# New orders for every engine of a two-layer attention and MoE kernel, new PSUM banks, and waits for loads at every step that needs them

## The reference

```python
x = x + L0_xattn(_layernorm(x), ctx, Wq, Wk, Wv, Wo, bo)     # 8 heads of 64
x = x + L0_ffn(_layernorm(x), w_gate, w1_e, w3_e, w2_e, w1_s, w3_s, w2_s)
                                # 16 experts of 64, best 4 within the best 2 of 4 groups; shared: 128
x = x + L1_xattn(_layernorm(x), ctx, Wq, Wk, Wv, Wo)         # 16 heads of 8
x = x + L1_ffn(_layernorm(x), router_w, experts_bias, w1, w3, w2, sw1, sw3, sw2)
                                # 8 experts of 256, best 2 by softmax; shared: 256
```

## Time and profile before

| | us |
|---|---|
| median of 3 runs (lowest to highest) | 231.48 (231.04 to 233.0) |
| span of the profiled execution | 230.0 |
| PE busy | 223.5 (97%) |
| DVE busy | 163.7 (71%) |
| ACT busy | 155.3 (68%) |
| POOL busy | 126.4 (55%) |

### The profile page before, as it was taken

How to read it: one execution, slowest core, us unless ns; L and a number is a source line. 1 busy time by engine, 2 the same in 40 slices (tenths; PEclk the granted TensorE clock), 3 DMA queues, 4 the chain that set the end, 5 groups by cost and what they waited for, 6 DMA issues and landing times.

```text
span 230.0 us, 4315 instructions
## 1 busy us (share of the span) xinstructions
PE 223.5 (97%) x1389; PEld 166.7 (72%) x1389; DVE 163.7 (71%) x480; ACT 155.3 (68%) x378; POOL 126.4 (55%) x127
## 2 busy tenths in 40 slices
PE   7999999999999999999999999999999999999994
PEld 3676765965889898889535563588878887888883
DVE  3589984788667863699948983564857775776874
ACT  2579999986679445672689778876365586745561
POOL 2765743899046937767492107209499400996540
PEclk9999999999999999999999999999999999999999
DMA  6890000000029925900600000028000003700002
GB/s 204 211 296 4 1 3 0 0 3 1 3 74 242 362 114 144 221 3 4 217 3 3 3 1 6 0 79 293 0 0 0 3 0 87 284 0 4 0 0 91
DMA packets 10172, 17.04 MB, mean 74 GB/s; under 512 B 3715, under 2 KB 5540, under 8 KB 9766
## 3 DMA queue, kind: packets, MB, share of 16 engines
q1 hardware_dynamic: 9926, 16.45, 23.5%
q10 hardware_dynamic: 224, 0.32, 0.4%
HBM read 16.08 MB, written 0.62 MB: 73 GB/s over the span
## 4 chain that ended last, share of the span: by engine, by line
PE 86%; ACT 6%; DVE 4%; POOL 2%; issue 1%; DVEq 0%; POOLq 0%
PE psum L1175 12%; PE psum L1179 11%; PE psum L1176 11%; PE psum L1348 7%; ACT prob L749 5%; PE psum L1410 5%; PE psum L1356 4%; PE psum L1358 3%; PE psum L1357 3%; PE psum L1466 3%; PE psum L1294 3%; PE psum L1306 3%; PE psum L1431 2%; PE psum L1270 2%; PE psum L1183 2%; PE psum L1454 2%
## 5 line engine op out<-in xcount | busy, mean ns | idle before, releaser
L703 POOL TENSOR_TENSOR act_s<-act_s,spread 128x512 f32<-128x512 f32 x35 | 44.3, 1293 | 20.2 <-DMA spread<-cw 14.5
L1175 PE MATMUL psum<-xT_hi,w_hi 128*128 128x512 f32 x108 | 43.9, 406 | 0.0
L1179 PE MATMUL psum<-xT_lo,w_hi 128*128 128x512 f32 x108 | 42.3, 392 | 0.0
L1176 PE MATMUL psum<-xT_hi,w_lo 128*128 128x512 f32 x108 | 42.2, 391 | 0.0
L798 ACT CAST q<-psum 128x512 fp32r<-128x512 f32 x35 | 20.4, 587 | 20.4 <-PE psum L1358 14.1
L1009 DVE TENSOR_TENSOR q<-psum,q 128x512 fp32r<-128x512 f32 x35 | 23.8, 687 | 13.5 <-ACT q L798 13.2
L788 ACT ACTIVATE act_s<-psum 128x512 f32<-128x512 f32 x39 | 23.0, 597 | 12.3 <-PE psum L1179 7.7
L1146 DVE TENSOR_REDUCE neg_max<-psum 128x2 f32<-128x308 f32 x64 | 26.2, 472 | 4.3 <-PE psum L1410 4.0
L703 POOL TENSOR_TENSOR hid<-hid,spread 128x512 f32<-128x512 f32 x13 | 16.6, 1296 | 18.9 <-DMA spread<-cw 14.6
L652 POOL TENSOR_TENSOR rstd<-vareps,minus_half 128x4 f32<-128x4 f32 x8 | 8.1, 1017 | 34.0 <-DVE vareps L910 34.0
L646 POOL TENSOR_TENSOR w_lo<-w_src,w_hi 128x768 fp32r<-128x768 f32 x12 | 21.7, 1830 | 8.3 <-ACT w_hi L718 8.3
(11 more groups left out here) (171 smaller groups left out, 469.6 us busy)
## 6 DMA issues: line engine op xcount, KB each, us to landing
spread<-cw SPq DMA_DIRECT2D x16, 256.0 KB, 4.9
spread<-cw SPq DMA_DIRECT2D x6, 512.0 KB, 5.7
w_src<-in_w SPq DMA_DIRECT2D x2, 1152.0 KB, 5.1
w_src<-in_w SPq DMA_DIRECT2D x1, 2304.0 KB, 11.6
spread<-cw SPq DMA_DIRECT2D x8, 128.0 KB, 3.0
w<-in_w SPq DMA_DIRECT2D x1, 576.0 KB, 6.6
out<-X SPq DMA_DIRECT2D x4, 128.0 KB, 1.8
wv<-in_wv SPq DMA_DIRECT2D x2, 192.0 KB, 4.7
```

Source lines behind the costliest of these rows:

```text
L703: pool.tensor_tensor(g, g, spread[:, slot, :], ALU.mult).then_inc(weighed, 1)
L1175: pe.matmul(dst, w_hi, xT_hi[:, b, :], start=True, stop=False)
L1176: pe.matmul(dst, w_lo, xT_hi[:, b, :], start=False, stop=False)
L1179: return pe.matmul(dst, w_hi, xT_lo[:, b, :], start=False, stop=True)
```

## The change

The whole of `PROGRAM` is rewritten: the same steps, in another order on all five engines, and PE's steps in other banks. SP's order differs in two places. In the first MoE layer a load stands ahead of the last of the five spreads of batch 0, and the load for the last layer's w2 stands one place further behind. The transpose of batch 0's expert weights (`cwT`) stood behind both halves of batch 1's `wo` and now stands between them. DVE rounds batch 0's `xT_lo` (`xT`) ahead of the statistics of batch 1's first tiles (the second `lnA`), where it stood behind them. Of the table these lines stand for the rest:

```diff
     "PE":
...
-        "pT.5 pT.3 pT.1 pT.2 k1.7 xT.6 k1.2 pT.4 pT.1 pT.6 gate.3 rest.1.6.4.5 pv pv pv pv h1.4 h1.6 wo.5 " +
-        "wo.1 cwT.3 h1.4 h1.3 h3.1 h3.4 h1.7 h3.1 xT.3 h3.0 h1.6 h3.5 gate.3 h3.7 h3.2 down.4 down down h1.1 " +
...
+        "h1.4 gate.3 pT.7 pT.0 pT.2 h3.6 rest.5.1.7.2 k1.0 pv pv pv pv wo.1 cwT.3 wo.2 h1.7 h1.5 h3.2 h3.4 h1.1 h1.3 " +
...
     "DVE":
-        "lnA sel lnA xT vf1 q q vf xT " + 9 * "score " +
...
+        "lnA xT lnA q q score score xT score score score score score vf1 norm q q score vf1 score score vs norm score " +
...
     "SP":
-        "store spread spread spread spread spread fetch store spread spread spread spread spread place_max " +
-        "fetch place_max place_max place_max store spread spread spread spread spread store spread spread " +
-        "spread spread spread out out out out ",
+        "store spread spread spread spread fetch spread store spread spread spread spread spread place_max place_max " +
+        "fetch place_max place_max store spread spread spread spread spread store spread spread spread spread spread " +
+        "out out out out ",
```

```diff
+        reached = {}
+
+        def need(eng, semaphore, n):
+
+            at = (id(eng), id(semaphore))
+            if n > reached.get(at, 0):
+                eng.wait_ge(semaphore, n)
+                reached[at] = n
+
         def wait_filled(eng, key):
 
             k, n, _ = uses[key]
-            eng.wait_ge(bank_ready[k], n)
+            need(eng, bank_ready[k], n)
...
         def wait_moved(eng, key):
 
-            eng.wait_ge(*reads_of(key))
+            need(eng, *reads_of(key))
...
+                    if s == 2:
+                        wait_moved(dve, ("y", 1, b))
...
                     moved(dve.tensor_tensor(xb, bank(key).rearrange("p (t d) -> p t d", t=T), xb, ALU.add), key)
-                    wait_moved(dve, key)
...
-            def product3(dst, w_hi, w_lo, s, b, first):
-
-
-                if first:
-                    pe.wait_ge(xT_rounded, position[("xT", s, b)])
+            def product3(dst, w_hi, w_lo, s, b):
+
+                need(pe, xT_rounded, position[("xT", s, b)])
                 pe.matmul(dst, w_hi, xT_hi[:, b, :], start=True, stop=False)
                 pe.matmul(dst, w_lo, xT_hi[:, b, :], start=False, stop=False)
-                if first:
-                    wait_moved(pe, ("xT", s, b))
+                wait_moved(pe, ("xT", s, b))
                 return pe.matmul(dst, w_hi, xT_lo[:, b, :], start=False, stop=True)
...
                 elif kind == "pT":
                     b, t, k = step[1:]
                     r = (b * T + t) % 2
-                    if k == 0:
-                        pe.wait_ge(prob_normed, position[("norm", b, t)])
+                    need(pe, loaded["ident"], 16)
+                    need(pe, prob_normed, position[("norm", b, t)])
```

More of the change, by code:

```diff
@@ L1190, in _ @@
                     p = step[1]
-                    if p == 0:
-                        pe.wait_ge(loaded["ctx"], 16 * N_CTX)
+                    need(pe, loaded["ctx"], 16 * N_CTX)
                     filled(pe.matmul(bank(step)[:, 0:B * CP], wk0[:, p * P:(p + 1) * P],
@@ L1195, in _ @@
                 elif kind in ("vf", "vf1", "vs", "vs1"):
+                    need(pe, loaded["ctx"], 16 * N_CTX)
                     if kind in ("vf", "vs"):
-                        if step == ("vf", 0):
-                            pe.wait_ge(loaded["ctxv"], 16)
+                        need(pe, loaded["ctxv"], 16)
                         w, k = wv0, CD
                     else:
-                        if step == ("vf1", 0):
-                            pe.wait_ge(loaded["kv1"], 16 * N_KV1)
+                        need(pe, loaded["kv1"], 16 * N_KV1)
                         w, k = wv1, CD + 1
@@ L1239, in _ @@
                     b, p = step[1:]
-                    if (b, p) == (0, 0):
-                        pe.wait_ge(lo_of["wq0"], 1)
+                    need(pe, lo_of["wq0"], 1)
                     c = slice(p * P, (p + 1) * P)
-                    filled(product3(bank(step), wq_hi0[:, c], wq_lo0[:, c], 0, b, p == 0), step)
+                    filled(product3(bank(step), wq_hi0[:, c], wq_lo0[:, c], 0, b), step)
                 elif kind == "scores":
@@ L1311, in _ @@
                     wait_moved(pe, ("xT", s, b))
-                    if (s, b) == (1, 0):
-                        pe.wait_ge(lo_of["gates"], 1)
+                    need(pe, lo_of["gates"], 1)
                     w = 2 * EXPERTS[s]
@@ L1332, in _ @@
                         pe.wait_ge(lo_of[name], w // CHUNK + 1)
-                    filled(product3(bank(step), hi[:, w, :], lo[:, w, :], s, b, False), step)
+                    filled(product3(bank(step), hi[:, w, :], lo[:, w, :], s, b), step)
                 elif kind == "down":
@@ L1382, in _ @@
                 elif kind == "qd":
-                    if step[1] == 0:
-                        pe.wait_ge(lo_of["wq1"], 1)
-                    filled(product3(bank(step), wq_hi1[:, :], wq_lo1[:, :], 2, step[1], True), step)
+                    need(pe, lo_of["wq1"], 1)
+                    filled(product3(bank(step), wq_hi1[:, :], wq_lo1[:, :], 2, step[1]), step)
                 elif kind == "q1":
```

54 lines of the change are left out of this document (23 added, 31 removed), and 57 rows, old and new, of the table PROGRAM.

## The result

The changed kernel takes 239.75 us in the median of 4 runs (237.09 to 749.74), the kernel before 231.39 us (231.04 to 233.0, 4 runs). The ratio is 1.030, 95% interval 1.023 to 1.038: slower, and above the forecast of 234.4 us and its range, which ended at 236.5. The run of 749.74 us, the profiled one, is left out of that ratio: its matmuls of 512 columns take 1.09 to 1.15 us each instead of 0.39 to 0.42, although its granted clock is given as full. The changed kernel was measured again, unchanged, beside the experiments. There it took 239.23 us (238.22 to 240.3, 4 runs), against 231.66 us for the kernel before, 7.6 us more (ratio 1.032, 1.027 to 1.037), and that profile is the one read here.

The account below looks back on a forecast made before the run. PE, busy 223.5 of 230.0 us, was taken as the bound. Lateness of 3.4 us less 0.5 gave 2.9, so a span of 232.9 us; with 1.48 up to the median, 234.4 us, range 228.9 to 236.5.

Parts of the forecast that it names:

- the largest term: Batch 0's last spread, queued behind the 2304 KB load, lands at 84.3 us and delays the last down: 2.8 us (0 to 4).
- Fewer waits: Fewer waits in the program: already met waits cost PE nothing, 0 taken, bounds 0 and a gain of 0.5 us.
- Start: Batch 1's statistics begin 1.4 us later, the first exponential about 0.6 us later; 0.2 us of loss kept (0 to 0.6).
- Second layer normalization: Batch 0: PE waits about 1.3 us at xT, less a vanished 0.54 us wait; net 0.6 to 0.9 us late.
- Weights and spread: Batch 0's router weights: cwT 0.9 us late (0.3 to 1.2), then the spread behind the load, 2.8 us (0 to 4).
- Third layer normalization: After batch 0's last down: xT starts at 93.0 us, PE 4.5 us late there at equal work.
- What comes back: Second attention: 1.1 of 4.5 us regained, 0.5 more through new banks (0 to 1.2), and 0 from 145 us on.
- The clock: Rival: PE's wait for hidden part 7 exceeds 2.6 us, the clock halves, ten products cost 2.3 us: 236.7 us, chance 0.02.
- A: Rival: the last spread lands before about 82.5 us, in time, and only small losses stay: 232.7 us, chance 0.16.
- B: Rival: faster; spread in time, early stalls hidden, no waits for banks from 97 to 145 us: 229.1 us, chance 0.15.
- D: Rival: the last spread costs about 1 us and later stages give it back: 231.5 us, chance 0.10.

Follow-up runs that it names:

- e1: The changed kernel measured once more, unchanged, for a clean profile: 239.23 us, ratio 1.032 to the kernel before.
- e4: The kernel before, its order and banks kept, with only the new way of writing waits: 231.66 us, ratio 1.0005.
- e5: e2 with PE's first xT behind all four kT and DVE's batch 1 statistics ahead of rounding xT_lo, as before: 234.77 us, ratio 1.0135.
- e2: The changed kernel with the 2304 KB load behind the fifth spread again, as before: 236.01 us, ratio 1.015 to the kernel before.
- e3: The kernel before with only the 2304 KB load moved ahead of the fifth spread: 236.09 us, ratio 1.018.
- e10: Old orders up to what the kernel before starts by 96 us, the changed kernel's orders behind: 233.94 us, ratio 1.011.
- e12: Old orders up to what the kernel before starts by 121 us, the changed kernel's orders behind: 233.83 us, ratio 1.0115.
- e8: The changed kernel with eight unused matmuls put into PE's wait ahead of hidden part 7's down: 238.17 us, ratio 1.027 to the kernel before.
- e13: The changed kernel with ACT's h1 activation, which calls a table load, moved ahead of the copy of the expert weights: 238.82 us, ratio 1.034.
- e14: The changed kernel with the fifth spread ahead of the load, e5's start and e13's ACT step: 236.04 us, ratio 1.019.
- e6: e2 with five later xT of PE moved behind one to three following steps: 242.36 us, ratio 1.045 to the kernel before.

## Why the prediction was wrong

The direction and the mechanism of the largest term were right, the sum wasn't: 7.6 us lost (e1) where 2.9 were forecast. Two steps failed. The prediction put the work from 145 us on at 0, "the products with the last layer's weights cover everything", and some 1.7 us are lost from 138 us on. And it gave a fall of the clock a chance of 0.02, on the condition that PE's wait exceed 2.6 us; the clock fell behind a wait of 1.92 us and beside one of 0.42, and costs about 2.1 us of the median. I compare PE's lateness at equal work, as the prediction did. (Starts of spans differ by up to 1.1 us between profiles, so only differences within one count.)

- **Fewer waits**: 0 forecast, 0 measured (e4).
- **Start**: 0.2 kept forecast. The changed kernel begins batch 0's scores at 14.19 us and the kernel before at 14.21, but with four projections of the context (1.5 us) still to do, and at 43 us it is 0.3 late. I had missed that `xT` now follows the first `kT`, a wait of 1.50 us. The two exchanges of e5 give back 0.6 us, and a wait of 1.42 us remains in it, so that the whole term isn't known.
- **Second layer normalization**: a wait of about 1.3 us at `xT` and 0.6 to 0.9 net forecast. Measured 1.02 us of wait, 1.3 us late there, and 0.5 to 0.9 a few steps on. Right.
- **Weights and spread**: POOL's seventh `weigh` forecast at 84.3 us, measured at 84.71 (no pause in the earlier trace rows); the `down` for part 7 started at 86.82. Forecast for the last one 87.6, measured 88.2, in part at the low clock. The sum took 2.2 us for the late spread, behind what it swallowed; measured are 1.8 us at full clock and 3.2 with the falls of the clock (e1 against e2), 3.0 and 4.4 in the old order (e3). Right in kind. That 84.3 was hit so well is in part luck. The prediction added its 0.9 us of lateness to the old place of `cwT`, 63.08, though by its own working PE now reaches it at equal work 61.3: it came at 62.06, 0.05 us behind the routing's last instruction on DVE, and not at 63.9 or later. The slow store took back 1.2 us of the 1.8 won, and from the first spread's issue to the landing of the last it took 19.0 us where the earlier trace rows give 17.9.
- **Third layer normalization**: 4.5 us late forecast; 6.2 measured, of which the low clock from 87.4 to 90.8 us made about 1.2. Without it 5.0.
- **What comes back**: forecast were 1.6 us up to 145 us and 0 behind it. In e2 the lateness is 3.9 us at 91 us and 2.9 at 138, so 1.0 did come back; in e1 it is 6.3 and 6.8, with `xT` of (2,1) waiting 0.42 us and the second low stretch between. Then the step that failed: from 138 us to the last matmul e2 goes from 2.9 to 4.6 us late and e1 from 6.8 to 8.6, and e10 and e12 lose 1.7 as well. All of it comes at the fourth layer normalization, in two places, at `xT` of (3,0) and where ACT stands 2.2 us for `xn` of batch 1. PE was busy throughout nearly all of it, but busy is not at pace: a `down` 0.46 us behind the matmul before it, not 0.23, hardly shows in PE's own rows.
- **The clock**: the second step that failed. 6 of the 7 runs of the changed kernel without the one of 749.74 us had a mean clock under 1.00, and the price was about 1.5 us a stretch, one or two in a run. The one fall that the earlier trace rows show, 2.6 us behind the last matmul, was no ground for that condition, and with 2.44 us of wait and no fall in e3 these runs give none in its place.

The sum by the measured parts, at full clock first: 237.09 us against 231.5 are 5.6 us, of which 1.8 are the spread, 0.6 the two exchanges of e5, about 1.7 the fourth layer normalization, and about 1.5 are left for the rest of the start and the layer normalizations between. The low stretches add 2.1 us (239.23 against 237.09), together 7.7 for the 7.6 us measured. The full-clock time of the changed kernel is a single run, and the parts overlap, so the split is not sharper than 1 us. Of the rivals A, B and D nothing was seen.

The fit of the Trainium skill (DMA: Bandwidth & Descriptors, "Anatomy of one DMA") would have had the last spread sooner than the rows: by a good 1 us as the prediction worked it out, by some 2 us if the whole load goes at the 312 GB/s of the earlier trace rows, 7.6 us instead of 5.4 (an estimate). It landed 0.4 us later than the figure from the rows. The ring order of the Trainium skill (DMA: Bandwidth & Descriptors, "Queues, rings and completion order") agrees with e3. By the Trainium skill (TensorE: Matmul & The Clock Gate, "Part 1: The HAM clock gate") idleness lowers the clock. The trace agrees with it behind the wait of 1.92 us, where in e8 the low stretch is gone with the wait; the profiled run of e3, at full clock behind 2.44 us, does not.

## What to carry to other kernels

A DMA that something waits for soon must not stand behind a large load in the same queue, however early both are issued: add up what the queue still has to move, and read from the rows when it will be empty. A new order can't win more than what PE now loses, but it can lose at every place where a step comes sooner than what it needs; where PE is the bound, look for its pace (start to start), not for its busy share, and follow the layer normalizations to the last one. When two medians differ by a few us, look at the granted clock of each run before giving all of it to the edit. And moving one step behind its neighbours to spare it a wait helped in none of the kernels here, since something else in the chain hung on it: look at what needs its result before moving it.

## What the runs showed of the hardware

- The queue of SP serves these DMAs in order of issue: with the 2304 KB load ahead of the last two DMAs of the spread, these landed at 83.4 to 84.7 us in six profiles, where the load itself landed at 83.4 before.
- The time at which the same transfers are through scatters by 2 us from one profiled kernel to another (20.6 to 22.6 us behind the transpose).
- The store of 32 KB was followed by the first spread after 1.83 to 1.85 us in eight kernels and after 2.36 to 3.11 us in nine with the new order ahead of it. A table load on ACT at the same moment doesn't explain it.
- The granted clock fell to one half behind a wait of PE of 1.92 us, and again 30.7 us behind the end of that stretch, beside a wait of 0.42 us; in e13 and e14, whose waits near 85 us are shorter or gone, the second fall is there as well (119.7 and 117.3 us). It did not fall behind a wait of 2.44 us in e3, nor beside the same wait of 0.43 us in e2.
- A low stretch of 3.4 us costs about 1.5 us in runs of the changed kernel, and one of 10.2 us goes with most of the 6.4 us that e6 lies above e2.
